# Node degrees and layer norms of a graph network's second layer, spread over other engines

## The reference, cut to what matters

```
h = jnp.maximum(_layernorm(x), 0.0)
x = x + L0(h, ..., src, dst)           # attention over the edges
h = jnp.maximum(_layernorm(x), 0.0)
x = x + relu(h @ Wv + bv) * gamma      # L1: a weight per node
h = jnp.maximum(_layernorm(x), 0.0)
x = x + (h + pi * segment_sum(h[src], dst)) @ W.T + b      # L2
h = jnp.maximum(_layernorm(x), 0.0)
x = x + L3(h, src, dst)                # Chebyshev terms, needs
deg = segment_sum(ones, src)           # the number of edges that leave each node
dis = where(deg > 0, rsqrt(max(deg, 1)), 0)
```

## Time and profile before

| | us |
|---|---|
| median of 3 runs | 1078.89 (1078.78 to 1079.4) |
| the profiled execution, its own time | 1081.17 |
| its span, first to last instruction | 1079.3 |
| TensorE busy | 950.7 (88%) |
| VectorE busy | 856.9 (79%) |
| ScalarE busy | 600.4 (56%) |
| GpSimd busy | 528.2 (49%) |

### The profile page before, as it was taken

How to read it: one execution, slowest core, us unless ns; L and a number is a source line. 1 busy time by engine, 2 the same in 40 slices (tenths; PEclk the granted TensorE clock), 3 DMA queues, 4 the chain that set the end, 5 groups by cost and what they waited for, 6 DMA issues and landing times.

```text
span 1079.3 us, 21468 instructions
## 1 busy us (share of the span) xinstructions
PE 950.7 (88%) x8293; PEld 568.1 (53%) x8293; DVE 856.9 (79%) x1304; ACT 600.4 (56%) x826; POOL 528.2 (49%) x522
## 2 busy tenths in 40 slices
PE   3887788888968999999999999969997899999995
PEld 2544454545542232322233333336686899999884
DVE  8899999999656999999999999978556463632476
ACT  8577777888347998989898988801000000001233
POOL 8697575754007999999999999800000000000000
PEclk9999999999897999999999999969998799999997
DMA  0010000000273122222222222210001010010211
GB/s 9 28 34 10 5 9 23 10 6 1 53 225 81 45 51 63 54 58 51 57 53 65 64 64 60 53 51 2 1 33 43 19 38 11 2 39 10 75 34 44
DMA packets 98577, 44.12 MB, mean 41 GB/s; under 512 B 85004, under 2 KB 96524, under 8 KB 98352
## 3 DMA queue, kind: packets, MB, share of 16 engines
q1 hardware_dynamic: 96784, 41.03, 14.4%
q0 software_dynamic: 1696, 1.74, 0.6%
HBM read 30.18 MB, written 12.56 MB: 40 GB/s over the span
## 4 chain that ended last, share of the span: by engine, by line
PE 66%; DVE 20%; issue 5%; ACT 3%; POOL 2%; DMA 2%; SPq 1%; DVEq 0%; ACTq 0%; POOLq 0%
PE PS L1294 19%; PE PS L1058 13%; PE PS L1068 12%; DVE oneS L410 7%; DVE mov L410 5%; PE PS L1302 4%; PE PS L1773 3%; PE PS L1047 3%; PE PS L547 2%; PE PS L539 2%; ACT Eb L1110 2%; PE PS L1285 2%; POOL Eb L971 1%; DVE Eb L1130 1%; PE PS L871 1%
## 5 line engine op out<-in xcount | busy, mean ns | idle before, releaser
L1110 ACT ACTIVATE Eb<-PS,small 128x1024 f32<-128x1024 f32 (+4 forms) x350 | 333.2, 1003 | 45.5 <-PE PS L1058 40.6
L1130 DVE TENSOR_TENSOR Eb<-Eb,PS 128x2048 f32<-128x2048 f32 (+4 forms) x175 | 341.8, 2011 | 19.1 <-POOL Eb L971 10.2
L971 POOL TENSOR_SCALAR Eb<-Eb 128x1024 f32<-128x1024 f32 (+4 forms) x350 | 318.8, 935 | 77.3 <-ACT Eb L1110 74.0
L1294 PE MATMUL PS<-hs,CT 128*128 128x192 f16 (+1 forms) x2500 | 214.1, 248 | 3.5 <-DVE SG L1539 1.6
L1294 PEld LDWEIGHTS PS<-hs,CT 128*128 128x128 f16 (+1 forms) x2500 | 208.6, 99 | 7.4 <-DVE SG L1539 2.3
L583 ACT ACTIVATE CT<-PS 128x500 f32 x313 | 175.7, 586 | 64.1 <-PE PS L547 62.3
L1058 PE MATMUL PS<-Qb,Kb 96*128 96x512 f16 (+3 forms) x700 | 180.2, 361 | 13.9 <-DMA Kb<-kd 10.7
L1068 PE MATMUL PS<-Eb,V 128*25 128x512 f32 (+3 forms) x1400 | 166.6, 548 | 0.8 <-DVE Eb L1130 0.8
L539 PE MATMUL PS<-mov,oneS 128*128 128x100 f16 x1565 | 126.1, 212 | 41.5 <-DVE mov L410 33.5
L1739 POOL MEMSET CT<- 1x384 f32 x1 | 0.4, 416 | 308.0 <-PE PS L1294 308.0
L1058 PEld LDWEIGHTS PS<-Qb,Kb 96*128 96x128 f16 (+1 forms) x700 | 42.4, 98 | 198.5 <-ACT Eb L1110 184.2
(11 more groups left out here) (279 smaller groups left out, 918.3 us busy)
## 6 DMA issues: line engine op xcount, KB each, us to landing
Kb<-kd SPq DMA_DIRECT2D x168, 96.0 KB, 2.4
qd<-QH SPq DMA_DIRECT2D x12, 192.0 KB, 2.9
kd<-QH SPq DMA_DIRECT2D x12, 192.0 KB, 3.2
hs<-t_d SPq DMA_DIRECT2D x12, 192.0 KB, 2.5
Qb<-qd SPq DMA_DIRECT2D x4, 384.0 KB, 4.2
CT<-x_d SPq DMA_DIRECT2D x1, 1200.0 KB, 7.7
x_d<-B SPq DMA_DIRECT2D x6, 192.0 KB, 1.9
t_d<-A SPq DMA_DIRECT2D x6, 192.0 KB, 1.8
```

The source lines that it names most:

```text
L971: g.tensor_scalar(e, e, EHI, ELO, ALU.min, ALU.max).then_inc(S("clamped"), 1)
L1110: a.activation(e, ps, ACT.Exp, scale=K.unsc[0:r, :]).then_inc(S("score_exp"), 1)
L1130: v.tensor_tensor(e, e, cn, ALU.mult).then_inc(S("weighed"), 1)
L1294: m = p.matmul(bank(t % FIRST)[0:r, 0:w], K.CT[:, a, 128 * t:128 * t + r], hs[:, a, :, :].rearrange("p k d -> p (k d)"), start=(a == 0), s ...
```

## The change

TensorE's sums of the rows of `K.CT` are removed, and bank 5 with them, so that `prop_first` now covers all six banks and `prop_rest` 19 tiles. The 25 row sums are made on two engines:

- In **proj**, VectorE sums tiles 0 to 5 with a reduction over 3136 elements each, one after each of the blocks 0 to 5. ScalarE sums tiles 6 to 12 in 14 halves of 1568 elements, as a copy into a scratch tile with its accumulator output: one after each of the seven `rows`, one after each of the seven blocks.
- In **prop**, ScalarE sums tiles 13 to 24 in 24 halves: two before the first root, two before the first `lin_copy`, two in each of the seven groups, six at the end.
- `degrees` now waits for all the halves and for L1's last norm, and adds the two columns of partial sums, `K.dp`.

L1's groups are handed round differently. The normalised values of both norms are made by GpSimd (`prop_gpsimd`: four `tensor_scalar` of 96 columns with two per-partition scalars, then one maximum over the group). The high half is written by ScalarE (`high`), which waits for GpSimd's second norm; VectorE's low half waits for ScalarE. VectorE keeps the statistics, the reciprocals (`ln_scale`), the gamma product, the addition and the low half. Roots are counted in one order, `LN_ORDER`.

```diff
+def source_half(a, K, scr, i):
+    t, k = SUMS_V + i // 2, i % 2
+    if i >= 2:
+        a.wait_ge(K.S("src_sum"), i - 1)
+    a.activation(scr[:, k, :], K.CT[:, t, HALF * k:HALF * k + HALF], ACT.Copy, accum_out=K.dp[:, t, k:k + 1]
+                 ).then_inc(K.S("src_sum"), 1)
@@ proj_vector
     for b in range(7):
         low(b)
         if b + 3 < 7:
             norm(b + 3)
+        if b < SUMS_V:
+            v.tensor_reduce(K.dp[:, b, 0:1], K.CT[:, b, 0:NP], AX.X, ALU.add).then_inc(step, own.up())
@@ proj_scalar, at the end of rows(b)
+        source_half(a, K, K.scr, b)
@@ proj_scalar, at the end of each block
         values(b)
         if b + 2 < 7:
             h_copy(b + 2)
+        source_half(a, K, K.scr, 7 + b)
@@ new
+def prop_gpsimd(g, K):
...
+    def norm(layer, out, c, slot, made):
+        n, o = tiles(c), 4 * slot
+        g.wait_ge(S("ln_scale"), LN_AT[layer, c])
+        for i in range(n):
+            g.tensor_scalar(out[:, i, :], K.B[:, 4 * c + i, :], K.mv[:, o + i, 0:1], K.rs[:, 2, o + i:o + i + 1],
+                            ALU.subtract, ALU.mult).then_inc(own.sem, own.up())
+        g.wait_ge(own.sem, own.n)
+        g.tensor_scalar(out[:, 0:n, :], out[:, 0:n, :], 0.0, None, ALU.max).then_inc(S(made), 1)
+
+    norm(1, K.SG[:, 0, :, :], 0, 0, "h1")
+    norm(1, K.SG[:, 1, :, :], 1, 1, "h1")
+    for c in range(NG):
+        if c + 2 < NG:
+            g.wait_ge(S("lin_turned"), c + 1)
+            norm(1, K.SG[:, c % 2, :, :], c + 2, c % 2, "h1")
+        norm(2, K.A[:, 4 * c:4 * c + tiles(c), :], c, 2 + c % 2, "h2")
@@ prop_tensor
-    source_sums(0)
     linear(0, K.SG[:, 0, :, :], 4)
     for g in range(NG):
         if g + 1 < NG:
             linear(g + 1, K.SG[:, (g + 1) % 2, :, :], tiles(g + 1))
-        source_sums(g + 1)
-        prop_first(0, g)
-    nxt = FIRST - 1
+        if g:
+            prop_first(0, g - 1)
+    prop_first(0, NG - 1)
+    nxt = FIRST
@@ prop_scalar
+    source_sums(2)
+    std1(1, 0)
+    std1(1, 1)
+    source_sums(2)
     lin_copy(0, 4)
     for g in range(NG):
         if g + 1 < NG:
             lin_copy(g + 1, tiles(g + 1))
+        if g:
+            high(g - 1)
+        if g + 2 < NG:
+            std1(1, g + 2)
+        std1(2, g)
+        source_sums(2)
+    high(NG - 1)
+    source_sums(6)
@@ prop_vector
+    for g in range(2):
+        l1_a(g)
+        ln_scale(1, g)
     for g in range(NG):
+        if g + 2 < NG:
+            l1_a(g + 2)
         l1_c(g)
+        if g + 2 < NG:
+            ln_scale(1, g + 2)
+        if g:
+            l1_d(g - 1)
+        ln_scale(2, g)
+    l1_d(NG - 1)
```

More of the change, by code:

```diff
@@ L601 @@
 TOP = float(2 ** 24)
+HALF = NP // 2
+SUMS_V = 6
+SUMS_ROWS = 14
+def source_half(a, K, scr, i):
[4 more added lines that the diff above has]
+                 ).then_inc(K.S("src_sum"), 1)
 def alloc_proj(K, st):
+    K.scr = K.sb(st, "scr", [128, 2, HALF], F16)
     sb = K.sb
@@ L694, in proj_vector @@
     v.memset(K.ones96[:, :], 1.0)
-    v.memset(K.V[:, :, :, 24:25].rearrange("p t h o -> p (t h o)"), 1.0)
+    v.memset(K.V[:, :, :, 24:25].rearrange("p t h o -> p (t h o)"), 1.0).then_inc(step, own.up())
     wr, sc = K.wr[:, :, :], K.sc
@@ L792, in proj_vector @@
     last_edges()
+    v.memset(K.dp[:, 0:SUMS_V, 1], 0.0).then_inc(step, own.up())
     for b in range(7):
@@ L1163, in attn_vector @@
     v.wait_ge(S("x1_sum"), 7)
-SRC_W = 20
-SRC_N = (NP + SRC_W - 1) // SRC_W
 FIRST_KEYS = ("l2", "p1", "p2", "p3")
+LN_ORDER = [(1, 0), (1, 1)] + [x for c in range(NG) for x in ([(1, c + 2)] if c + 2 < NG else []) + [(2, c)]]
+LN_AT = {x: i + 1 for i, x in enumerate(LN_ORDER)}
 def alloc_prop(K, st):
     sb = K.sb
+    K.scr2 = sb(st, "scr2", [128, 2, HALF], F16)
     K.A = sb(st, "A", [128, NT, D], F32)
@@ L1226 @@
 PI = 3.1415927410125732
+def prop_gpsimd(g, K):
+    S, own = K.S, K.own["g"]
+    def norm(layer, out, c, slot, made):
[13 more added lines that the diff above has]
+        norm(2, K.A[:, 4 * c:4 * c + tiles(c), :], c, 2 + c % 2, "h2")
+    g.wait_ge(S("h2"), NG)
 def prop_sync(q, K):
@@ L1297, in prop_mm @@
             m.then_inc(S("propped"), 1)
[L1299 to L1305, removed]
     def prop_first(k, g):
-        for t in range(FIRST if k else FIRST - 1):
+        for t in range(FIRST):
             if g == 0 and k:
@@ L1390, in lin_copy, with high, source_sums @@
         a.activation(K.HT[0:96, 0:128 * n], K.bank(6)[0:96, 0:128 * n], ACT.Copy).then_inc(S("lin_kept"), 1)
-    std("ln1", 1, 0, 0)
+    def high(g):
+        sl = slice(4 * g, 4 * g + tiles(g))
+        a.wait_ge(S("h2"), g + 1)
+        a.activation(K.HP[0][:, sl, 0, :], K.A[:, sl, :], ACT.Copy, scale=UP).then_inc(S("high"), 1)
+    halves = iter(range(SUMS_ROWS, 2 * (NT - SUMS_V)))
+    def source_sums(n):
+        for _ in range(n):
+            source_half(a, K, K.scr2, next(halves))
+    source_sums(2)
+    std1(1, 0)
+    std1(1, 1)
+    source_sums(2)
     lin_copy(0, 4)
@@ L1432, in degrees @@
     def degrees():
[L1433 to L1436, removed]
+        v.wait_ge(S("src_sum"), 2 * (NT - SUMS_V))
+        v.tensor_tensor(K.degs, K.dp[:, :, 0], K.dp[:, :, 1], ALU.add).then_inc(step, own.up())
         v.wait_ge(S("h2"), 7)
+        v.wait_ge(step, own.n)
         v.tensor_scalar(pf[:, 0, :], K.degs, 1.0, None, ALU.max).then_inc(S("deg_max"), 1)
```

44 lines of the change are left out of this document (20 added, 24 removed).

## The result

The changed kernel takes 1102.52 us in the median of 4 runs (1102.26 to 1103.36), against 1079.07 for the kernel before (1078.78 to 1079.4). The ratio is 1.021, with a 95% interval of 1.0197 to 1.0222: slower, as forecast, but by 23.4 us where 8.3 were forecast, and beyond the range that ended at 1097. The profiled execution took 1103.36 us with a span of 1101.5.

What follows compares the result with a forecast made beforehand. TensorE's sums were taken to bound L1, and the chain of low half, store and high half the projections. +12.8 and -4.5 made +8.3 us on 1078.9, so 1087.2 us; range for 8 in 10: 1081 to 1097.

Steps and rivals of the forecast that it cites:

- Term 1: Projections: six VectorE reductions, 3.3 us apart, lengthen its path; +12.8 us.
- rival 3: Projections: the 16-bit reduction reads several elements a cycle; no change at 1.8 us apart, faster from 1.55 down; chance 0.10.
- Term 2: L1: TensorE's sums go, GpSimd's norms set a loop of 6.7 us a group, passes start earlier; -4.5 us.
- I take 0.5, and 2.75 for the norm: L1, GpSimd's norm: 0.5 us for an operation of 96 columns, 2.75 us for the whole norm.
- Rival 1: L1: GpSimd's norm slow because it and VectorE get in each other's way; 1112 us, or about 1096; chance 0.16.
- Rival 2: L1: GpSimd's norm quick, 1.7 us, loop 4.8 us; 1079.7 us, no change; chance 0.13.
- Rival 4: ScalarE's half sums: the accumulator costs an instruction, 0.2 us a half; +1.5 to +2.5, about 1089; within the forecast's 0.61.

Runs made afterwards that it cites:

- third: The changed kernel without ScalarE's 24 half sums in L1 (their degrees left out): 1091.58 us, ratio 1.0105.
- sixth: The change with L1's norms and high halves back on VectorE, the six reductions and all 38 halves kept: 1096.76 us, ratio 1.0161.
- seventh kernel: The change with GpSimd's maximum written as a minimum with 1e38, then a maximum with 0: 1094.82 us, ratio 1.0144.
- eighth kernels: The seventh kernel with GpSimd's normalisation also written as product then sum, its bias made by VectorE: 1085.65 us, ratio 1.0055.
- fourth kernel: The change with GpSimd's maximum followed by a minimum with 1e38 in the same instruction: 1107.21 us, ratio 1.0242.
- the first experiment: The changed kernel without VectorE's six row reductions in the projections (their degrees left out): 1090.18 us, ratio 1.0091.
- the test loop: The kernel before with twelve forms of small GpSimd instructions, four of each, added beside L2 on a scratch tile: 1081.71 us, measured once.

## Why the prediction was wrong

The whole was slower, as forecast, and the path through the projections and the loop of L1 is the one that the forecast described. The price of GpSimd's norm was too low, and with it L1's term has the wrong sign.

- **Term 1, the reductions: right within about a microsecond, in part by luck.** 3.42 us forecast, 3.41 measured; from the first low half to the end of the last it is 32.65 us, 32.6 forecast; leaving the reductions out gives 12.3 us back, 12.8 forecast. The Trainium skill (VectorE: DVE Perf Modes, The perf-mode tier table) has a reduction at one element a cycle for every type; the 16-bit row of 3410 ns for 3136 elements agrees, and rival 3 fell by the same row. Between the two executions the stage grew by 14.0, 1.2 more than the term. Seen from the first column sum, the first low half comes 2.5 us later than before (26.97 us behind it instead of 24.43), where 0.4 was forecast, and from the end of the last low half to the first exponential it is 1.9 us less (8.19 instead of 10.12), where 1.0 was forecast. That the last low half started at 332.18, near the forecast's 332.7, is luck: the stage had begun 2.7 us earlier. The late first low half does not come with the change each time. In the third, sixth, seventh and eighth kernels, whose projections are the change's, it comes 23.9 to 24.4 us behind the column sum, and the stage from there to the first exponential takes 64.7 to 65.2 us instead of the change's 67.8 (53.8 before), so 10.9 to 11.4 more than before; the fourth kernel has 26.9 and 67.8. Counted from the start of the program, the first exponential comes 10.4 to 12.9 us later in all six than before. The two with the long stage have TensorE at the half clock early. This is the same stretch in the change and in the seventh kernel, with the columns of the earlier trace rows; the third number from the end is the granted clock:

```profile
295.00:300.00 5.00, 5.00 (x20) 3.88 (x19) 1.38 (x11) 1.75 (x4) 0.00 (x0) 0.50 0.00 0
```

```profile
295.00:300.00 5.00, 5.00 (x29) 3.32 (x28) 2.38 (x12) 4.46 (x10) 0.00 (x0) 1.00 0.00 0
```

The attention's +1.8 comes with the reductions: without them, in the first experiment, it takes 377.4 us from the first exponential to the meeting of prop, as before. Its beginning runs at the half clock for longer in the change: the granted clock is 1.00 from 335.5 to 345.5 us before, whose first exponential is at 329.36, and still 0.50 from 340.5 to 350.5 us in the change, with 340.71. What the clock alone costs there was not separated.
- **Term 2, L1: the step that failed is "I take 0.5, and 2.75 for the norm".** The loop's build, 1.1 us of hand-overs and two norms, is what the trace shows. A norm took 3.95 to 4.5: 0.69 for each operation of 96 columns instead of 0.5, and 1.17 for the maximum instead of 0.51. The remaining passes start 78.8 us behind the meeting where the forecast had 64.4 (771.3 less 706.9), 14.4 later, and the half clock behind them cost 1.3 instead of 2.5. With that the term is +8.7 instead of -4.5, 13.2 of the 13.9 us by which the spans' difference (22.2) was missed. When both forms were written as the cheap pairs, the whole kernel came to 1085.65, 1.5 below the forecast of 1087.2, and 5.6 above the kernel before beside it, where 8.3 were forecast; a norm is 2.4 to 2.7 us in it.
- **The error in method** was to take a price per column from the lines nearest in width, L971 and L1743, without looking at their operations in the code. Both are cheap pairs; the norm is neither, and the maximum is one operation alone. The right row was in the earlier trace rows: L219 is one operation alone, 128 columns in 0.54 us. Less the fixed 0.19 that is 2.7 ns a column, or 1.24 us for 384, where 1.17 was measured. I used that row for the operations of 96 columns and not for the maximum.
- **Rival 1 had the size right (3.6 a norm gave 1096, 5.2 gave 1112) and the main cause wrong.** It blamed VectorE beside GpSimd. But the lone maximum takes 1.17 us both in L1's second norm and in the test loop, and the seventh kernel takes 7.7 us out without moving anything on VectorE. A smaller part is as rival 1 said. The first norm of a group takes up to 0.5 us more than the second (3.22 and 2.70 in the rows above, and two of its maxima 1.48 and 1.51). It is not the statistics: beside them a row takes its usual time. The longer rows are those that run beside VectorE's addition (L1572) or its low half (L1581), in the change and in the fourth and seventh kernels alike. GpSimd's rows and then VectorE's, in the change:

```profile
735.17 2.72 POOL L1260 TENSOR_SCALAR SG<-B,mv,rs 128x96 f32<-128x96 f32 x4 [2.79 <-DVE rs L1560]
737.97 1.48 POOL L1263 TENSOR_SCALAR SG<-SG 128x384 f32<-128x384 f32 x1
```

```profile
735.30 0.74 DVE L1519 BATCH_NORM_STATS2 bns<-B 128x6 f32<-128x96 f32 x4
737.87 0.56 DVE L1572 TENSOR_TENSOR B<-B,TR 128x384 f32<-128x384 f32 x1
```

  Added up over the loop of the change this is about 2.4 us, an estimate from what such rows take above 2.70 and 1.17 (0.69 and 0.45 in the group of one tile). It is read from what ran at the same time; no run takes it out alone.
- **Rival 2** (GpSimd near line rate, with the Trainium skill, GPSIMD Engine Reference, When to use GPSIMD, beside it) is refuted for one operation alone, 1.17 us for 384 columns or 3.0 ns each, and holds only for the two pairs, 0.56 us or 1.4 ns each.
- **Rival 4 was right in kind and not in size:** the accumulator costs an instruction of its own, 0.19 us, but the next one starts 0.09 us after it. Two halves are 1.49 us apart instead of the 1.45 assumed, and the last six take 8.96 where 8.7 were forecast. That is 0.3 us on the path, where the rival had 1.5 to 2.5.
- **TensorE's idle time before the passes** was forecast as about 10 us and was 9.81, and the price of the half clock behind it as 2.5; the first hundred products took 9.71 us instead of 8.42, so 1.3.

## What to carry to other kernels

Before work is moved to GpSimd, its price must be read from a row with the same operations in the same order, not from one of the same width; if there is none, both ends of the range belong in the sum, and one test loop settles it. Written in the cheap forms the norms are worth moving to GpSimd (11.1 us under the same norms on VectorE), in the others not (5.8 us over them). For the row sums two things counted. One is where they go: 12.3 us on VectorE between the low halves, nothing on ScalarE beside them. The other is who waits for them: the same 50 halves cost 8 us when the degrees were wanted at once, and the kernel gained 3.5 when they were wanted only by L2's first group. An engine that idles beside the path (ScalarE's roots had waited 53.4 us for VectorE) took work for nothing wherever nobody waited for what stood behind it.

## What the runs showed of the hardware

- GpSimd's `tensor_scalar` on 384 32-bit columns: 1.17 us for one operation alone (maximum or product), 0.56 for minimum then maximum or product then sum, 1.50 for maximum then minimum. The order of the same two operations alone makes 0.94 us for maximum and minimum. With two per-partition scalars on 96 columns: 0.775 for difference then product, 0.525 for product then sum.
- The same instruction of GpSimd takes up to 0.34 us more while VectorE adds two 32-bit tensors (L1572): 1.48 and 1.51 us instead of 1.17. Beside VectorE's statistics it does not (four operations of 96 columns in 2.70 to 2.72 us).
- A ScalarE activation with an accumulator output is followed by a second instruction of 0.19 us that reads the accumulator.
- TensorE is at the half clock for much of L1 once its sums are gone, in the kernels that beat the kernel before too: in the one with the maximum in ScalarE's copy a product takes 2.02 us at 745.60 and 1.13 at 752.76. What that costs was not separated.
